# Layer 2's entry moved into its output stage, its denominators inverted per head, and preparation spread over the engines

## The reference

```python
x = norm(x + linear_attention(x))        # layer 1
x = norm(x + expert_attention(x))        # layer 2, the one that changes
x = norm(x + gated_softmax_attention(x)) # layer 3
x = norm(x + ternary_mlp(x))             # layer 4
```

```python
values = einsum('bhne,ehdk,bnd->bhnk', gm, value_experts, x)
attn   = softmax(causal(q * SCALE @ k.T))
out    = attn @ values
out    = einsum('bhne,ehkd,bhnk->bhnd', gm, output_experts, out).sum(heads)
```

## Time and profile before

| engine | busy us | share of the span |
|---|---|---|
| PE | 3274.7 | 89% |
| PEld | 2349.5 | 64% |
| DVE | 1997.1 | 54% |
| ACT | 1494.3 | 40% |
| POOL | 771.8 | 21% |

### The profile page before, as it was taken

One profiled execution on the slowest core, in us unless ns is written; L12 is line 12 of the kernel. 1 busy time (PEld: TensorE's weight loads), 2 busy tenths in 40 slices (PEclk: granted clock), 3 DMA queues, 4 the chain that ended last, 5 costly groups with the idle time before them and its releaser, 6 DMA issues. The chain is left out here.

```text
span 3695.5 us, 50581 instructions
## 1 busy us (share of the span) xinstructions
PE 3274.7 (89%) x18322; PEld 2349.5 (64%) x18322; DVE 1997.1 (54%) x3358; ACT 1494.3 (40%) x2706; POOL 771.8 (21%) x724
## 2 busy tenths in 40 slices
PE   7896989889889888889898699898998979999998
PEld 4554745876459754687457664645556458888887
DVE  4345844668446764459545565674756643333333
ACT  2321144421444134441344247465564634444443
POOL 1121500653007420265004410101001011111111
PEclk9897999999999999999999899999999989999999
DMA  5102100201011100111002101000010040000000
GB/s 183 48 34 70 46 1 1 78 32 39 1 31 47 47 23 1 51 40 35 23 1 70 66 1 13 13 2 24 2 23 3 2 167 12 12 12 17 7 7 12
DMA packets 175604, 119.82 MB, mean 32 GB/s; under 512 B 116609, under 2 KB 157825, under 8 KB 171905
## 3 DMA queue, kind: packets, MB, share of 16 engines
q1 hardware_dynamic: 175360, 116.54, 10.7%
HBM read 99.18 MB, written 28.31 MB: 34 GB/s over the span
## 5 line engine op out<-in xcount | busy, mean ns | idle before, releaser
L874 POOL TENSOR_TENSOR l2c_rlo<-l2c_routed,l2c_rhi 128x512 fp32r<-128x512 f32 x256 | 347.1, 1369 | 914.5 <-ACT l2c_rhi L900 875.6
L1410 ACT ACTIVATE l3b_prob<-sums 128x512 f32<-128x512 f32 (+3 forms) x768 | 333.3, 493 | 203.7 <-PE sums L1343 164.6
L1659 PE MATMUL sums<-l_uhi,l_h 128*128 128x512 f32 x1024 | 405.8, 396 | 0.0
L1659 PE MATMUL sums<-l_ulo,l_h 128*128 128x512 f32 x1024 | 405.6, 396 | 0.0
L806 DVE TENSOR_REDUCE l2b_mx<-sums 128x1 fp32r<-128x1024 f32 (+7 forms) x256 | 193.0, 757 | 315.7 <-PE sums L687 313.8
L713 PE MATMUL sums<-l2b_prob,l_vx 128*128 128x512 f32 (+3 forms) x768 | 309.3, 513 | 38.6 <-DVE l_oT L798 23.8
L743 ACT ACTIVATE l2b_prob<-sums 128x512 f32<-128x512 f32 (+3 forms) x384 | 181.2, 489 | 316.2 <-PE sums L704 311.5
L984 PE MATMUL sums<-l2c_ohi,l2c_rhi 128*128 128x256 f32 x1024 | 295.8, 289 | 12.7 <-POOL l2c_rlo L874 11.8
L984 PE MATMUL sums<-l2c_ohi,l2c_rlo 128*128 128x256 f32 x1024 | 293.4, 287 | 0.0
L984 PE MATMUL sums<-l2c_olo,l2c_rhi 128*128 128x256 f32 x1024 | 293.3, 286 | 0.0
L1338 PE MATMUL sums<-l_qst,l_kst 64*128 64x512 f32 (+3 forms) x768 | 279.0, 428 | 14.9 <-ACT l3b_prob L1410 6.4
(11 more groups left out here) (259 smaller groups left out, 7513.6 us busy)
## 6 DMA issues: line engine op xcount, KB each, us to landing
l_ve<-ve SPq DMA_DIRECT2D x34, 512.0 KB, 3.8
l_oe<-oe SPq DMA_DIRECT2D x16, 1024.0 KB, 6.0
l2c_word<-weights_copy SPq DMA_DIRECT2D x32, 352.0 KB, 3.9
sb_nx<-sums SPq DMA_DIRECT2D x10, 1024.0 KB, 5.6
weights_copy<-h SPq DMA_DIRECT2D x2, 4096.0 KB, 25.7
l_qst<-l3b_peak SPq DMA_DIRECT2D x512, 0.5 KB, 2.0
l_h<-weights_copy SPq DMA_DIRECT2D x2, 4096.0 KB, 23.5
sb_nx<-tokens SPq DMA_DIRECT2D x5, 1024.0 KB, 5.3
```

Of the source, the lines that this page charges most:

```text
L874: pool.tensor_tensor(rlo[:, i % RT, :], routed[:, i % RT, :], rhi[:, i % RT, :].bitcast(F32), ALU.subtract).then_inc(s.routed_lo, 1)
L1410: act.activation(prob[:, i % RB, j, a, 0:hi - lo], bank(m.ps, part % SCORE, 0, hi - lo), ACT.Exp, scale=SCALE1).then_inc(s.exp_ready, 1)
L1659: run(lambda out, a, x, first, last: pe.matmul(out, a, x, start=first, stop=last))
```

## The change

Five edits go together.

1. *Denominators.* ACT copies the head's output (`head_out`), DVE inverts all 64 denominator rows of 1024 (`den_out`) out of PSUM, POOL multiplies the two in `oT`. `dens`, its DMAs and its transposes go. The gates, no longer divided, are split by DVE and transposed by PE at the start of attention and copied to `gmT` by ACT.
2. *Entry.* Transposes, gate logits and gate steps of the next pass stand in the output stage, at fixed block numbers, in bank 7; the mask products have 3 banks instead of 4. The statistics and scaling go there too. For the first pass they stand in `fetch_first`. The rounding to `xhi` is ACT's.
3. *Value layout.* The 512 columns are ordered feature first, then expert, so that the sum over experts reads without a gap. POOL's halving steps read 4, 2 and 1 of every 8.
4. *Preparation.* `memset` of `vx`, `sel` and the masks go to POOL, layer 3's casts to ACT; two unused constants go.
5. *Fewer blocks.* The block ahead of layer 1 goes; its loads and casts stand in layer 1's `fetch_first`. The last sums of the output stage are read for the first four tiles one block earlier.

```diff
-def fetch_first(nc, m, s, src, load, prepare):
+def fetch_first(nc, m, s, src, load, begin=None, by_tensor=None, by_vector=None, by_scalar=None, by_pool=None):
...
+    def entry_turn(pe, t):
+        if t:
+            pe.wait_ge(s4.xT_ready, t)
+        for c in range(KC):
+            last = pe.transpose(bank(m.ps, ENTRY, c * P, (c + 1) * P), m.nx[:, t, c * P:(c + 1) * P], m.ident[:, :])
+        last.then_inc(s4.transposed, 1)
...
+    def by_tensor(pe):
+        for t in range(NT):
+            pe.wait_ge(s0.nx_ready, t + 1)
+            entry_turn(pe, t)
+        pe.wait_ge(ld.weights, 16 * 7)
+        gate_logits(pe)
...
-                        dve.tensor_reduce(vx[:, t, h, vcol(h)], vm[:, n % VM, :].rearrange("p (e k) -> p k e", e=NE),
-                                          AX_X, ALU.add).then_inc(s.v_ready, 1)
+                        dve.tensor_reduce(vx[:, t, h, vcol(h)], by_key(vm[:, n % VM, :]), AX_X, ALU.add).then_inc(s.v_ready, 1)
...
-                        step(pool.tensor_tensor(slot[:, 0:256], slot[:, 0:256], slot[:, 256:512], ALU.add))
+                        step(pool.tensor_tensor(slot[:, :, 0:4], slot[:, :, 0:4], slot[:, :, 4:8], ALU.add))
...
                         if x == 3:
-                            warm(pe, 6, 8)
+                            turn_gates()
+                            warm(pe, 6, 4)
...
-                def den_out(h):
+                def head_out(h):
                     act.wait_ge(s.pv_mm, NT * (h + 1))
                     if h >= 2:
-                        act.wait_ge((s.even_den_out, s.odd_den_out)[h % 2], 16 * (h // 2))
-                    act.copy(den[den_row(h), h % 2, :], bank(m.ps, PV, 0, T, den_row(h))).then_inc(s.den_read, 1)
+                        act.wait_ge(s.o_ready, h - 1)
+                    act.copy(oT[vcol(h), h // 2, :], bank(m.ps, PV, 0, T, vcol(h))).then_inc(s.o_read, 1)
...
-                def head_out(h):
+                def den_out(h):
                     dve.wait_ge(s.pv_mm, NT * (h + 1))
-                    dve.tensor_copy(oT[vcol(h), h // 2, :], bank(m.ps, PV, 0, T, vcol(h))).then_inc(s.o_read, 1)
+                    if h >= 2:
+                        dve.wait_ge(s.o_ready, h - 1)
+                    dve.reciprocal(rden[vcol(h), h % 2, :], bank(m.ps, PV, 0, T, dens(h))).then_inc(s.den_read, 1)
...
-                fetch_stats(dve, m, s)
-                fetch_norm(dve, m, s)
-                head_out(H0 - 1)
+                den_out(H0 - 1)
...
+                for h in range(H0):
+                    pool.wait_ge(s.o_read, h + 1)
+                    pool.wait_ge(s.den_read, h + 1)
+                    part = oT[vcol(h), h // 2, :]
+                    pool.tensor_tensor(part, part, rden[vcol(h), h % 2, :], ALU.mult).then_inc(s.o_ready, 1)
...
+        MASKS = 3
+        turn_at = {10 + 3 * t: t for t in range(NT)}
+        LOGITS_AT, GATES_FROM, EXP_AT, SD_AT, NORM_FROM = 35, 37, 38, 5, 6
...
+                    if i == 1:
+                        fetch_stats(dve, m, sf)
+                    if i == NORM_FROM:
+                        fetch_rstd(dve, m, sf)
+                    if NORM_FROM < i <= NORM_FROM + NT:
+                        fetch_scale(dve, m, sf, i - NORM_FROM - 1)
+                    if 0 <= i - GATES_FROM < len(gates):
+                        gates[i - GATES_FROM]()
...
-                dve.wait_ge(s.out_mm, len(blocks))
                 for t in range(NT):
+                    dve.wait_ge(s.out_mm, len(blocks) - (t < NT // 2))
...
-        def prepare(dve):
-            dve.memset(vx[:, :, :, :], 1.0).then_inc(ld.ones, 1)
...
+        def by_pool(pool):
+            pool.memset(vx[:, :, :, :], 1.0).then_inc(ld.ones, 1)
+
+        def by_scalar(act):
+            act.wait_ge(ld.weights, 16 * 16)
+            act.copy(select[:, :, :, :, :].rearrange("p a b r n -> p (a b r n)"), given[:, :]).then_inc(ld.select, 1)
```

More of the change, by code:

```diff
@@ new lines, in entry_take, with gate_logits @@
+    def entry_take(act, t):
+        act.wait_ge(s4.transposed, t + 1)
+        act.copy(xT[:, :, t * P:(t + 1) * P], bank(m.ps, ENTRY, 0, D).rearrange("p (c q) -> p c q", c=KC)).then_inc(s4.xT_ready, 1)
+    def gate_logits(pe):
+        pe.wait_ge(s4.xT_ready, NT)
+        for t in range(NT):
+            for c in range(KC):
+                last = pe.matmul(bank(m.ps, ENTRY, t * 64, t * 64 + 64), xT[:, c, t * P:(t + 1) * P], wg[:, c, :],
+                                 start=(c == 0), stop=(c == KC - 1))
+        last.then_inc(s4.logits, 1)
@@ L497, in _ @@
             def _(pe):
-                entry_transpose(pe, m, s)
-                for t in range(NT):
-                    pe.wait_ge(s.xT_ready, t + 1)
-                    for c in range(KC):
-                        last = pe.matmul(bank(m.ps, 7, t * 64, t * 64 + 64), xT[:, c, t * P:(t + 1) * P], wg[:, c, :],
-                                         start=(c == 0), stop=(c == KC - 1))
-                last.then_inc(s.logits, 1)
                 for n, (h, t) in enumerate(order):
@@ L527, in _ @@
                 expert_hi(0)
-                entry_copy(act, m, s, xT)
-                act.wait_ge(s.exp_in, 1)
-                act.activation(e[:, :], z[:, :], ACT.Exp).then_inc(s.exp_out, 1)
+                for t in range(NT):
+                    cols = slice(t * P, (t + 1) * P)
+                    act.copy(xhi[:, :, cols], xT[:, :, cols]).then_inc(s.x_hi, 1)
                 for h in range(1, H0):
@@ L774, in _ @@
                     if k2 == 0 and 1 <= h2 < H0:
[L775 to L778 removed]
+                        head_out(h2 - 1)
+                    if x == 3:
+                        for n in range(NH):
+                            act.wait_ge(s.gates_turned, n + 1)
+                            act.copy(gmT[:, n * HALF:(n + 1) * HALF], bank(m.ps, 3 + n)).then_inc(s.gmT_ready, 1)
+                head_out(H0 - 1)
             @block.vector
@@ L888, in _ @@
                 expert_hi(0, 1)
-                for n in range(NH):
-                    act.wait_ge(s.gmT_mm, n + 1)
-                    act.copy(gmT[:, n * HALF:(n + 1) * HALF], bank(m.ps, 5 + n)).then_inc(s.gmT_ready, 1)
                 for i in range(len(blocks)):
@@ L909, in _ @@
             def _(dve):
-                step = Chain(dve, s.chain)
+                gates = gate_steps(dve)
                 def expert_lo(c, j):
```

244 lines of the change are left out of this document (127 added, 117 removed).

## The result

The changed kernel takes 3900.16 us (median of 4 runs, 3892.93 to 3902.45), the kernel before 3698.42 us beside it: ratio 1.0543, interval 1.0525 to 1.0561, +201.7 us. The forecast was 3903.

The account below looks back on a forecast made before the run. TensorE, in order, was taken to bound nearly all of layer 2, with no slack in the read at a head's end. The terms summed to +204 us on the 3698.5 us median: 3903 us, range 3815 to 3980.

Parts of the forecast that it names:

- A: Attention, head's end: PE waits for a 6.55 us reciprocal instead of a 1.22 us copy, 28 times; +148.3 us.
- B: Attention, after each of 28 longer stops: PE runs 3.4 to 6.3 us at the low clock; +50 us.
- C: Hand-over from attention to output stage: 6.9 us lost by reciprocal and multiply, 6.3 gained by dropped steps; +2 us.
- D: Output stage: next entry's PE products, crowded VectorE steps and contention add 10.1 us a pass; +40 us.
- E, passes 2 to 4: Value stage: no stop for gate steps and a contiguous sum, so attention starts 11.5 us earlier each pass; -34.6 us.
- E, first pass: First value stage: entry and gates in the first block, then waits for POOL; +6 us.
- F: Attention's start: turned gates' copies delay first maxima by 1 us, table reload goes (0.8); +1 us in four passes.
- G: Layer starts: layer 1's tokens load 3.9 us earlier, layer 3's preparation off VectorE saves 4.7; -8.6 us.
- (1): Rival, attention: the clock comes back or never falls after the stops, no clock loss; 3853 us, chance 0.14.
- (2): Rival, output stage: the crowd decides, 20 to 25 us a pass, each gate step waiting for POOL; 3953 us, chance 0.10.
- (3): Rival, value stage: POOL's sums with gaps bound the values, 30 us a pass; 4023 us, chance 0.08.
- (4): Rival, faster: the reciprocal of this form runs like the copy; -15 us, 3683 us, chance 0.05.

Follow-up runs that it names:

- x3_warm: The changed kernel with 22 (30 for two heads a pass) extra unused TensorE products in each stop, before its wait for the reciprocal: 3847.21 us, ratio 1.0405.
- x1_copy: The changed kernel with VectorE copying each head's row of denominators instead of inverting it, the inversion left out: 3682.15 us, ratio 0.9969.
- z1_oldlayout: The changed kernel with value weights in their old expert-by-expert order and masks, sums and halvings in the old shapes: 3903.23 us, ratio 1.057.
- x5_first: Against the changed kernel with its inversion in eight chunks (3727.0 us): denominator and head copies go first at a head change, one more chunk copied; 3705.21 us.

## Why the prediction was right

The sum was right to 2 us (+204 predicted, +201.7 measured). By its own steps, the measured side from the two traces' first and last instructions of each stage, except where the table names a run:

| step | predicted | measured |
|---|---|---|
| A, stop at a head's end | +148 | +145 (x3_warm less x1_copy) |
| B, clock after it | +50 | +49 to +51 (after less x3_warm) |
| C, hand-over | +2 | -1 |
| D, output stage | +40 | +53 |
| E, passes 2 to 4 | -35 | -36 |
| E, first pass | +6 | +3 |
| F, attention's start | +1 | -5 |
| G, layer starts | -9 | -8 |
| rest of layers 3 and 4 | 0 | +2 |

*A* was mis-sized by 3 us at most: the reciprocal is 6.555 us where 6.55 was worked out from two other shapes, and the rule "all of it is PE's" held in 28 of 28 places. *B* came at the 50 taken for it, and in the way predicted: behind the 28 stops the clock stood at the 1.2 GHz level for 3.1 to 5.8 us of PE's work, 4.3 in the mean, where 3.4 to 6.3 was put. The clock cost 12.3 us in a stretch of 214.5, and 49 of 3900 us over the kernel, 1.3%. The page "TensorE: Matmul & The Clock Gate" of the Trainium skill, section "What's actually happening", puts the ramp penalty under 1% of a typical kernel's span; this kernel, with 28 stops, lies above that, and the term was rightly kept in the sum.

*D* was mis-sized: 10.1 us a pass was predicted, 13.2 came (the four stages grew by 58.2 us, less 5.3 that the early last sums gave: predicted as 1.3 a pass, they end 1.33 us sooner behind the last product). PE's own work was right (5.4 against 5.75). The crowd with contention was put at 6.0 and is about 8 (3.0 of clock, 5.2 of idle): no clock loss had been put in this stage. With the entry's steps spread over free blocks the crowd nearly goes. That VectorE waits for POOL in this stage can be read from the trace: L145 took 821 ns in the mean where the same form takes 334 in the earlier trace rows (2.67 us for eight), and L115, on 8 elements per row, 1166 ns, where it takes 171 in layer 3. Two of them beside the POOL operation during which they began:

```profile
1204.81 1.28 POOL L957 TENSOR_TENSOR l2c_rlo<-l2c_routed,l2c_rhi 128x512 fp32r<-128x512 f32 x1 [0.17 <-ACT l2c_rhi L980]
1207.78 1.30 POOL L957 TENSOR_TENSOR l2c_rlo<-l2c_routed,l2c_rhi 128x512 fp32r<-128x512 f32 x1 [1.68 <-ACT l2c_rhi L980]
```
```profile
1204.95 1.17 DVE L115 TENSOR_SCALAR sb_sd<-sb_sd 128x8 f32<-128x8 f32 x1
1207.88 1.35 DVE L145 TENSOR_SCALAR sb_nx<-sb_nx,sb_moments,sb_rstd 128x256 f32<-128x256 f32 x1
```

Each ends 0.03 to 0.16 us after that POOL operation, and so do the other five scalings of this stage that began during one; the two that met none took 0.41 and 0.40 us. This fits the exclusive lock of the port pair that the Trainium skill describes in "SBUF — State Buffer", section "Who interferes with whom". How much of D it is, no run isolates.

*E* had the right sum for passes 2 to 4, and its parts hold: the first value product comes 3.3 to 4.7 us earlier (without the 1.33 of above), the products' stretch is shorter by 4.6 to 6.1, and attention's first projection follows it 2.5 us sooner. What PE waits for last before the first value product is VectorE's remainder of x (L622, 34.6 us in three places), but POOL's remainder of the weights sets it, as predicted: in the second pass POOL's runs from 843.07 to 845.41, and L622, which takes 0.41 us when POOL is idle, begins at 843.33 and ends at 845.70. Of the reasons, the contiguous sum (0.69 instead of 1.07 us, as predicted) turned out to be no visible part of the gain (z1_oldlayout). The first pass was over-sized: measured from the start of layer 1 its first value product is 8.4 us later, but its products then run 2.8 us shorter and attention starts 2.5 sooner. *C* was over-sized by 3 us: the stop that stands for it, 9.4 us four times (L1050), is the inversion, the multiply and the block's end, and weighs as much as what went. *F* was too, by 6: the copies of the turned gates do delay the first row maximum by 1.1 us, as predicted (PE waits 3.5 us for them, L848, in place of a wait of 3.2 before), but from there to the first product with the values it takes 14.4 us instead of 16.4, at a granted clock of 0.86 instead of 0.79 (second pass). Why the clock is up sooner there is not shown. *G* was right in layer 1 (4.7 us earlier; 3.9 predicted) and near in layer 3 (about 3; 4.7).

The error of D (+13) and those of A, C, E and F (-3, -3, -4 and -6) nearly cancel, so that the sum is right to 2 us is partly luck.

Rivals: (1) fell with the 0.55 row. (2), the crowd as deciding term, fell: 53, not 90. (3) fell entirely: POOL's sums with gaps take 727, 399 and 308 ns, together 1.43 us, no more than the 1.5 us of before. (4) fell with the 6555 ns; x1_copy, in which the step does run like a copy, took 3682 us (3687 by the ratios) where the rival said 3683.

## What to carry to other kernels

Ask of every instruction moved between engines what it stands between. If it reads the accumulator that the bound engine wants back, its whole length is paid at each turn; here the lower clock behind each stop added a third to that. Read the bank out with the cheapest instruction, first in its queue, and do the arithmetic from SBUF where the queue has room; and cost elementwise work by elements per partition, so that work on 64 partitions is joined in pairs. Before a faster form of a step is credited, check whether its engine was what the bound engine waited for: the new value layout saved 13 us of VectorE per stage and nothing of the time that shows.

## What the runs showed of the hardware

- Stops of 3.1 to 5.7 us cost the clock as much as stops of 5.8 to 8.3 (PE busy 162.1 and 161.2 us for the same 613 products; 150.0 with stops of 0.5 to 3.0). The clock also fell with no single wait over 1.72 us (x5_first: 0.61 and then 0.53, right behind the wait of 1.72).
- A reciprocal's time followed the elements per partition, not the number of partitions: 6555 ns for 64x1024, 3355 for 64x512, 3353 for 128x512, 939 for 128x128 and 896 to 942 for 64x128.
- VectorE operations with SBUF alone as source and target (L115, L145) that began while GpSimd ran one in the output stage ended 0.03 to 0.16 us after it: 1.17 us for 8 elements per row, up to 1.35 for 256, against 0.17 and 0.40 without. The multiply with one input in PSUM (L1015) began beside GpSimd too, at 1218.13, and took its usual 0.68 us.
- Sums with gaps: the stride of 64 cost VectorE 1077 against 686 ns for the same elements (z1_oldlayout and after). GpSimd's three halvings took 727, 399 and 308 ns with gaps and 736, 461 and 322 without.
